# Three rounded passes for the query projections, the first context transposed in two halves, and a shorter first layer norm in a fused Perceiver layer

## The reference

```python
x = x + xattn(layernorm(x), ctx, ctx, Wq, Wk, Wv, Wo)   # 32 query heads, 8 key heads of 16, softmax over 512 keys
x = x + attn(layernorm(x), Wq, Wk, Wv, Wo)              # self-attention, rotary, causal, over 32 tokens
x = x + (layernorm(x) @ dequantised_3bit_W.T + bias)
```

## Time and profile before

| | |
|---|---|
| median of 3 runs | 363.48 us (362.62 to 363.76) |
| the profiled execution | 363.82 us |
| its span in the trace | 362.0 us |
| TensorE busy | 340.7 us, 94% |
| VectorE busy | 234.7 us, 65% |
| ScalarE busy | 201.6 us, 56% |
| GpSimd busy | 104.3 us, 29% |

### The profile page before, as it was taken

How to read it: one execution, slowest core, us unless ns; L and a number is a source line. 1 busy time by engine, 2 the same in 40 slices (tenths; PEclk the granted TensorE clock), 3 DMA queues, 4 the chain that set the end, 5 groups by cost and what they waited for, 6 DMA issues and landing times.

```text
span 362.0 us, 8407 instructions
## 1 busy us (share of the span) xinstructions
PE 340.7 (94%) x2958; PEld 243.1 (67%) x2962; DVE 234.7 (65%) x420; ACT 201.6 (56%) x371; POOL 104.3 (29%) x195
## 2 busy tenths in 40 slices
PE   8999778999999999999999999998798989999996
PEld 4755545777777777777777777775456748875664
DVE  2977655676676667666766766666856237886652
ACT  4543244567576675666675766758766522275310
POOL 1431812133131240331322412403103141551410
PEclk9999988999999999999999999999999999999999
DMA  7980497685876777869759686989600000000002
GB/s 282 394 94 4 92 208 172 159 101 162 141 138 149 110 177 159 109 168 175 99 154 163 116 173 125 205 196 122 84 0 2 2 0 2 1 2 0 2 29 87
DMA packets 35820, 41.25 MB, mean 114 GB/s; under 512 B 15136, under 2 KB 30496, under 8 KB 33696
## 3 DMA queue, kind: packets, MB, share of 16 engines
q1 hardware_dynamic: 35360, 40.74, 55.0%
q10 hardware_dynamic: 432, 0.13, 0.2%
HBM read 24.07 MB, written 1.05 MB: 69 GB/s over the span
## 4 chain that ended last, share of the span: by engine, by line
PE 82%; DVE 8%; DMA 2%; SPq 2%; ACT 2%; POOL 2%; issue 1%; ACTq 0%; DVEq 0%; POOLq 0%
PE b_d L1025 9%; PE b_s L1046 8%; PE b_c L1084 8%; PE b_v L1000 4%; PE b_c L1230 4%; PE b_v L1002 4%; PE b_v L1001 4%; PE b_k L1002 4%; PE b_k L1000 4%; PE b_k L1001 4%; PE b_x L972 3%; PE b_t L972 3%; DMA kstack<-kparts 2%; PE b_c L1215 2%; PE b_c L1111 2%; PE b_v L1051 2%
## 5 line engine op out<-in xcount | busy, mean ns | idle before, releaser
L758 DVE TENSOR_REDUCE negmax<-b_s 128x1 f32<-128x512 f32 x128 | 88.1, 688 | 67.1 <-PE b_s L1046 65.5
L610 ACT ACTIVATE region<-b_c 128x512 f32<-128x512 f32 x128 | 76.4, 598 | 60.9 <-PE b_c L1084 58.5
L1046 PE MATMUL b_s<-kstack,qstack 96*128 96x512 bf16 x128 | 50.2, 392 | 7.9 <-DVE negmax L758 3.5
L1084 PE MATMUL b_c<-qstack,kstack 108*128 108x128 bf16 x512 | 50.8, 222 | 0.3 <-ACT qstack L564 0.3
L1084 PEld LDWEIGHTS b_c<-qstack,kstack 108*128 108x128 bf16 x512 | 32.7, 98 | 26.5 <-issue 15.7
L469 POOL TENSOR_TENSOR mwide<-negmax,zeros 128x4 bf16<-128x4 f32 x32 | 6.4, 199 | 119.0 <-DVE negmax L758 119.0
L1025 PE MATMUL b_d<-region,vaug 128*17 128x128 f32 x1024 | 34.2, 274 | 0.0
L1000 PE MATMUL b_v<-cT_h,wkv_h 128*128 128x512 f32 x64 | 31.6, 494 | 0.0
L460 POOL TENSOR_TENSOR kparts<-kres,zeros 128x512 bf16<-128x512 f32 x16 | 18.9, 1179 | 44.0 <-DVE kres L743 44.0
L1000 PE MATMUL b_k<-cT_h,wkv_h 128*128 128x512 f32 x64 | 30.5, 476 | 0.0
L1025 PEld LDWEIGHTS b_d<-region,vaug 128*17 128x17 f32 x1024 | 25.2, 97 | 3.4
(11 more groups left out here) (395 smaller groups left out, 678.0 us busy)
## 6 DMA issues: line engine op xcount, KB each, us to landing
cx<-in_ctx_dram SPq DMA_DIRECT2D x16, 1024.0 KB, 5.2
kstack<-kparts SPq DMA_DIRECT2D x96, 128.0 KB, 4.6
qstack<-region SPq DMA_DIRECT2D x76, 32.0 KB, 3.6
xs<-in_x_dram SPq DMA_DIRECT2D x1, 1024.0 KB, 8.0
region<-in_L_xattn_Wq_dram SPq DMA_DIRECT2D x1, 1024.0 KB, 10.2
cx<-in_L_xattn_Wo_dram SPq DMA_DIRECT2D x8, 128.0 KB, 5.0
cx<-in_L_attn_Wq_dram SPq DMA_DIRECT2D x1, 1024.0 KB, 5.3
region<-in_L_attn_Wo_dram SPq DMA_DIRECT2D x8, 128.0 KB, 7.6
```

The lines of the kernel that those rows point to most:

```text
L610: nc.scalar.activation(pT[:, g], b_c[g % 2][:].rearrange("p (a n) -> p a n", a=KT), ACT.Exp, scale=SCALE).then_inc(exp_ready, 1)
L758: nc.vector.tensor_reduce(negmax[:, n % 2, g:g + 1], b_s[:], AX, ALU.max, negate=True).then_inc(max_ready, 1)
L1046: nc.tensor.matmul(b_s[:], qstack[0:STACK, g, n % 4], kstack[0:STACK, n % 4, g], start=True, stop=True).then_inc(s_ready, 1)
L1084: last = nc.tensor.matmul(b_c[g % 2][:, P * a:P * a + P], kstack[0:ROWS, m % 4, g, P * a:P * a + P], qstack[0:ROWS, g, m % 4], start=True, ...
```

## The change

Four edits, all in the openings.

1. The query projection takes three passes in the rounded format instead of one in fp32: `wq_h` by `xhT_h`, `wq_l` by `xhT_h`, `wq_h` by `xhT_l`, each over four chunks. The weights' high parts are copied into head order by ScalarE (chunk 0) and POOL (1, 2, 3); the low parts are subtracted by VectorE (0, 1) and POOL (2, 3), POOL's after all four tiles are normalised. The transposed rows' high parts are copied on ScalarE and their remainders subtracted on VectorE. The new operands lie in `wT_h`, `wT_l`, `swq_h` and `swq_l`, which are free until much later.
2. Context 0 is loaded in two halves of its row blocks, and transposed in two halves, with `warm(8)` ahead and `warm(2)` between, instead of `warm(14)`; both `warm(4)` are gone. The projections of context 0 wait chunk by chunk.
3. Epsilon becomes the bias of the square root.
4. The order changes. TensorE does query 0 ahead of the value transposes and of context 1, then queries 1 to 3 together, then chunks 2 and 3 of context 1. ScalarE and VectorE take those two chunks after all query parts, ScalarE also after its two DMA issues; VectorE unpacks the last piece (`unpack(5)`) after them, and does context 0's key remainder behind the row remainders.

```diff
+        wq_h, wq_l = (w[:].rearrange("p c (r n) -> p c r n", r=R) for w in (wT_h, wT_l))
+        xhT_h, xhT_l = swq_h, swq_l
+        b_rows = (b_c[1], b_t, b_x, b_s)
...
@@ SyncE, opening
+                halves = ctx_d[0].rearrange("(p a) d -> p a d", a=KT)
+                sp.dma_start(cx[:, 0, 0:2], halves[:, 0:2]).then_inc(first_half, 16)
                 sp.dma_start(wkv_raw[:, 0], xwk_d.rearrange("(c p) m -> p c m", p=P)).then_inc(wk_loaded, 16)
-                load_ctx(0, 0)
+                sp.dma_start(cx[:, 0, 2:4], halves[:, 2:4]).then_inc(ctx_loaded[0], 16)
...
@@ POOL, opening
+            nc.gpsimd.memset(eps[:], EPS).then_inc(eps_ready, 1)
...
                 pool.wait_ge(xwq_loaded, 16)
+                for c in (1, 2, 3):
+                    nc.gpsimd.tensor_copy(in_heads(wq_h, c), from_heads(xwq, c)).then_inc(wq_high[c], 1)
+                pool.wait_ge(xh_ready, TILES)
                 for c in (2, 3):
-                    nc.gpsimd.tensor_copy(wq_dg[:, c].rearrange("p r (d g) -> p r d g", g=G),
-                                          xwq[:, c].rearrange("p (g r d) -> p r d g", g=G, r=R)).then_inc(wq_ordered, 1)
+                    pool.wait_ge(wq_high[c], 1)
+                    nc.gpsimd.tensor_tensor(in_heads(wq_l, c), from_heads(xwq, c), in_heads(wq_h, c).bitcast(F32),
+                                            ALU.subtract).then_inc(wq_ready[c], 1)
...
@@ ScalarE, opening
-                act.wait_ge(ln1_var, 1)
-                nc.scalar.activation(rstd[:], mv[:, :, 1], ACT.Sqrt).then_inc(ln1_std, 1)
+                act.wait_ge(ln1_aggr, TILES)
+                act.wait_ge(eps_ready, 1)
+                nc.scalar.activation(rstd[:], mv[:, :, 1], ACT.Sqrt, bias=eps[:]).then_inc(ln1_std, 1)
                 act.wait_ge(xwq_loaded, 16)
-                nc.scalar.activation(wq_dg[:, 0].rearrange("p r (d g) -> p r d g", g=G),
-                                     xwq[:, 0].rearrange("p (g r d) -> p r d g", g=G, r=R), ACT.Copy).then_inc(wq_ordered, 1)
+                nc.scalar.activation(in_heads(wq_h, 0), from_heads(xwq, 0), ACT.Copy).then_inc(wq_high[0], 1)
+                for t in range(TILES):
+                    act.wait_ge(xh_transposed, t + 1)
+                    nc.scalar.activation(xhT_h[:, :, P * t:P * t + P], b_rows[t][:].rearrange("p (c n) -> p c n", c=C),
+                                         ACT.Copy).then_inc(xhT_high, 1)
                 act.wait_ge(v_chunk, C)
                 nc.scalar.activation(vT[:], b_v[:], ACT.Copy).then_inc(vT_ready, 1)
...
+                query_high(0)
                 context(1, 0)
                 context(1, 1)
-                query_high(0)
-                context(1, 2)
                 query_mid(0)
-                query_high(1)
-                context(1, 3)
-                query_mid(1)
-                for r in (2, 3):
+                for r in (1, 2, 3):
                     query_high(r)
                     query_mid(r)
                 act.wait_ge(q_mid, R)
                 first_queries_part(act, 1, 0, 1, first_queries)
+                context(1, 2)
+                context(1, 3)
                 key_high(1, 0)
...
@@ VectorE, opening
-                nc.vector.tensor_scalar(mv[:, :, 1], mv[:, :, 1], EPS, None, ALU.add).then_inc(ln1_var, 1)
...
+                for c in (0, 1):
+                    dve.wait_ge(wq_high[c], 1)
+                    nc.vector.tensor_tensor(in_heads(wq_l, c), from_heads(xwq, c), in_heads(wq_h, c).bitcast(F32),
+                                            ALU.subtract).then_inc(wq_ready[c], 1)
+                for t in range(TILES):
+                    dve.wait_ge(xhT_high, t + 1)
+                    nc.vector.tensor_tensor(xhT_l[:, :, P * t:P * t + P], b_rows[t][:].rearrange("p (c n) -> p c n", c=C),
+                                            xhT_h[:, :, P * t:P * t + P].bitcast(F32), ALU.subtract).then_inc(xhT_ready, 1)
                 key_residue(0, 0)
-                dve.wait_ge(xwq_loaded, 16)
-                nc.vector.tensor_copy(wq_dg[:, 1].rearrange("p r (d g) -> p r d g", g=G),
-                                      xwq[:, 1].rearrange("p (g r d) -> p r d g", g=G, r=R)).then_inc(wq_ordered, 1)
+                query_residue(0)
                 copy_values(0, 0)
                 context(1, 0)
                 context(1, 1)
+                query_low(0)
                 unpack(0)
                 unpack(1)
-                query_residue(0)
-                context(1, 2)
-                query_low(0)
+                query_residue(1)
+                query_low(1)
                 unpack(2)
                 unpack(3)
-                query_residue(1)
-                context(1, 3)
-                query_low(1)
-                unpack(4)
                 query_residue(2)
                 query_low(2)
-                unpack(5)
+                unpack(4)
                 query_residue(3)
                 query_low(3)
+                context(1, 2)
+                context(1, 3)
+                unpack(5)
                 key_residue(1, 0)
...
@@ TensorE
-                    if not looped(trip) and (m, c) == (1, 1):
-                        pe.wait_ge(xhT_ready, 1)
+                    if not looped(trip) and m == 1:
+                        pe.wait_ge(xhT_ready, TILES)
...
             def first_queries_of(r):
-                pe.wait_ge(xhT_ready, TILES)
-                pe.wait_ge(wq_ordered, C)
-                count(pe, q_res, r - 1)
-                for c in range(C):
-                    last = nc.tensor.matmul(b_c[r % 2][:], wq_dg[:, c, r], xhT[:, c], start=(c == 0), stop=(c == C - 1))
+
+                for i, (w, x, w_done) in enumerate(((wq_h, xhT_h, wq_high), (wq_l, xhT_h, wq_ready), (wq_h, xhT_l, wq_high))):
+                    pe.wait_ge((xhT_high, xhT_high, xhT_ready)[i], TILES)
+                    if i == 0 and r > 1:
+                        pe.wait_ge(q_res, r - 1)
+                    for c in range(C):
+                        pe.wait_ge(w_done[c], 1)
+                        last = nc.tensor.matmul(b_c[r % 2][:], w[:, c, r], x[:, c], start=(i == 0 and c == 0), stop=(i == 2 and c == C - 1))
                 last.then_inc(q_summed, 1)
...
             def opening():
                 pe.wait_ge(zeros_ready, 1)
-                warm(14)
+                warm(8)
                 pe.wait_ge(ident_loaded, 16)
-                first_context(0)
-                first_context(1)
-                first_context(2)
-                first_context(3)
-                warm(4)
-                pe.wait_ge(wk_split, 1)
+                pe.wait_ge(first_half, 16)
                 for c in range(C):
-                    project(0, 0, c, 0)
-                pe.wait_ge(wv_split, 1)
+                    first_context(c, (0, 1))
+                warm(2)
+                pe.wait_ge(ctx_loaded[0], 16)
                 for c in range(C):
-                    project(0, 1, c, 0)
-                warm(4)
+                    first_context(c, (2, 3))
+                pe.wait_ge(wk_high, 1)
+                first_projection(0)
+                pe.wait_ge(wv_high, 1)
+                first_projection(1)
...
+                first_queries_of(0)
                 pe.wait_ge(vT_ready, 1)
...
                 next_context(1, 0)
                 next_context(1, 1)
-                first_queries_of(0)
+                for r in range(1, R):
+                    first_queries_of(r)
                 next_context(1, 2)
-                first_queries_of(1)
                 next_context(1, 3)
-                first_queries_of(2)
-                first_queries_of(3)
                 for which in range(2):
                     for c in range(C):
                         project(1, which, c, 0)
```

More of the change, by code:

```diff
@@ L197, in perceiver @@
         scratch = kstack[:, 2:4].rearrange("p a g n -> p (a g n)").bitcast(F32)
+        eps = sb("eps_sb", [P, 1])
         qbytes = scratch[:, 0:3 * NTRIP].bitcast(I32).rearrange("p (n k) -> p n k", k=3)
         qvals = scratch[:, 3 * NTRIP:11 * NTRIP].bitcast(I32).rearrange("p (n k) -> p n k", k=8)
-        wq_dg = qstack[:].rearrange("p g i n -> p (g i n)").bitcast(F32).rearrange("p (c r n) -> p c r n", c=C, r=R)
+        wq_h, wq_l = (w[:].rearrange("p c (r n) -> p c r n", r=R) for w in (wT_h, wT_l))
+        xhT_h, xhT_l = swq_h, swq_l
         bits = scratch[:, 11 * NTRIP:15 * NTRIP].bitcast(I32).rearrange("p (k n) -> p k n", k=4)
@@ L251, in perceiver @@
             [sem(f"{name}{i + 1}") for i in range(2)] for name in ("ln_stats", "ln_aggr", "ln_var", "ln_std", "ln_rstd", "xn_ready"))
+        wq_high, wq_ready = ([sem(f"{name}{c}") for c in range(C)] for name in ("wq_high", "wq_ready"))
         ctx_loaded = [sem(f"ctx_loaded{i}") for i in range(2)]
@@ L307, in wait_queries, with in_heads, from_heads @@
                 eng.wait_ge(qstack_loaded[m % 4], 16 * SLOTS * (m // 4))
+        def in_heads(w, c):
+            return w[:, c].rearrange("p r (d g) -> p r d g", g=G)
```

(41 more changed lines are left out.)

20 lines of the change are left out of this document (7 added, 13 removed).

## The result

The changed kernel takes 366.58 us (median of 9 runs, 365.25 to 367.06) against 363.48: a ratio of 1.0077, with a 95% interval of 1.0053 to 1.0101. It is slower by 3.1 us, where 1.9 us of gain was forecast. Its profiled execution took 366.26 us with a span of 364.5, so it is 2.5 us longer than the span of 362.0 shown before.

The account below looks back on a forecast made before the run. TensorE, busy for 94% of the span, was taken as the bound, the change touching only the opening. Slot 1 0.35 us earlier plus 1.55 of half clock gone gave -1.9: 361.6 us against 363.48, range 358.2 to 365.2.

Parts of the forecast that it names:

- The mechanism named as likeliest: Opening: VectorE can't follow, TensorE waits 3.75 us for chunk 2, half clock follows, slot 1 at 55.7; 361.6 us, chance 0.42.
- The price of the passes: Query projections: 2.73 us a query in rounded products, 2.8 us of TensorE saved; queries 1 to 3 take 8.2.
- the first context: Context 0 in halves, fewer warming products: first chunk at about 7.4 against 7.45, taken as nothing, bounds -0.4 and +0.5.
- the normalising beside the copies: Layer norm: four tiles take 2.19 us on VectorE, not blocked by POOL's copies; rows end at 16.45.
- the half clock before slot 0: After TensorE's wait for chunk 2: 3.1 us at half clock, 1.55 us lost; slot 0 begins at 44.8.
- the tail: From slot 1 on nothing is touched, TensorE is busy to 97%, and the shift passes to the end.
- query 0 done: End of query 0's third pass: 23.2 us instead of 22.6, bounds 21.4 and 24.5.
- if the clock rises one stretch later: First context: bound of +0.5 us on its start, should TensorE's clock rise later.
- no turns: Rival on weight subtractions: no exclusion between VectorE and POOL, query 0 ends at 21.4; 358.9 us, chance 0.18.
- The rival "slower": Query 0's second and third pass: both POOL subtractions precede VectorE's second, TensorE's clock falls; 365.1 us, chance 0.14.
- That sign of the rival: A low clock between 20 and 27 us, named as what would show the slower rival (chance 0.14).
- The landing rival: Before slot 1: last key DMA issued at 47.2 takes 8.9 us again, slot 1 at 56.1; 363.5 us, chance 0.21.

Follow-up runs that it names:

- e4: Changed kernel with fifteen zero products in TensorE's wait for chunk 2 of context 1: 363.40 us, ratio 0.9985.
- e5: Changed kernel with ten zero products in TensorE's wait for the first self-attention rows at 261 us: 364.93 us, ratio 1.0033.
- e6: Kernel before with ten zero products in TensorE's wait for the first self-attention rows: 363.57 us, ratio 1.0010.
- e3: Changed kernel with chunks 2 and 3 of context 1 back between the queries on all three engines: 364.31 us, ratio 1.0013.
- e7: Changed kernel with GpSimd's three weight copies held until the rows are normalised: 367.98 us, one run.
- e8: Changed kernel with context 0 in one load and chunks 2 and 3 of context 1 back between the queries: 363.02 us, ratio 0.9980.
- e10: e8 with context 3's load issued early and ten zero products in the wait at 261 us: 358.94 us, ratio 0.9876 to the kernel before.
- e12: Kernel before with context 3's load issued early and ten zero products in the wait at 261 us: 359.45 us, ratio 0.9873.
- e9: Kernel before with context 3's load issued before SyncE waits for the query parts: 361.02 us, ratio 0.9944.

## Why the prediction was wrong, step by step

The mechanism named as likeliest was there: VectorE as the bound, a wait of 3.5 us (3.75 forecast) for chunk 2, a half clock after it, no wait for the keys and full clock into slot 1. That no key was waited for was forecast rightly: landed by 54, and by 55.8 at the latest in the trace. The price of the passes was right too: queries 1 to 3 take 8.3 us (26.57 to 34.87), where 8.2 was forecast. The sign was wrong because four terms were too small: the first context and the normalising beside the copies, which were taken at no loss, the half clock before slot 0, and the tail. In the profiled executions the forecast of -1.9 and the measured +2.5 differ by 4.4 us: 2.6 at 64 us and 1.8 in the tail. Of the 2.6, 2.4 are slot 1's start, and the rest is that the half clock of the kernel before behind slot 1 gave back 1.3 us instead of 1.55.

| step | forecast | measured | difference |
|---|---|---|---|
| first eviction | 7.65 | 8.59 | +0.94 |
| layer norm, from statistics to reciprocal | -0.38 | -0.34 | +0.04 |
| four tiles normalised | 2.19 | 3.42 | +1.23 |
| the four subtractions | 4.65 | 4.6 | 0 |
| query 0 done | 23.2 | 25.5 | +2.3 |
| low part of chunk 2 | 38.7 | 40.74 | +2.0 |
| from there to slot 0 | 6.1 | 7.14 | +1.0 |
| slot 0 | 10.9 | 10.17 | -0.7 |
| slot 1 begins | 55.7 | 58.11 | +2.4 |
| behind it | 0 | 1.8 | +1.8 |

*First context.* Taken at nothing, bound +0.5. The argument was that the same bytes had to be in as before. The runs show that they came in later (212 GB/s from 2 to 4 us against 320; key weights used at 6.48, not 3.88; second half at 8.1) and that two-part transposing costs 1.1 us even when they don't. The fall-back "if the clock rises one stretch later" was priced at +0.5; where it happened the eviction was at 9.5 to 9.9.

*Copies and normalising.* This was argued away in the rival "no turns": the normalising beside the copies "wasn't blocked". The row of four was a sum, and hid that one tile had taken 0.82 us and the others 0.53. In the old order the two overlapped for 0.5 us; in the new one the three copies (14.4 to 17.9) run beside most of the normalising (15.25 to 18.67). The Trainium skill's page "SBUF — State Buffer" (section "Who interferes with whom") says that VectorE's copy, cast and tensor_scalar can contend with GpSimd too, when they run in a mode that uses both ports, and not only instructions with two SBUF inputs. The prediction left that clause unused. The trace agrees with it (1.92 us alone, 3.42 beside three copies), though no run here shows the mode that the instruction ran in.

*The half clock before slot 0.* Priced at 3.1 us from two rows, it lasted 5.3 us after TensorE had resumed, 2.6 us of lost time instead of 1.55. e4 shows that this and nothing else stood between the low part of chunk 2 and slot 0.

*The tail.* "From slot 1 on nothing is touched" held for every instruction and failed for the clock. The wait at 261 us is the same 2.27 us in both, and filling it takes 1.65 us off one median and nothing off the other (e5, e6). No term or rival was made for it.

The rival "slower" had the right sign with the wrong place: GpSimd didn't take both its turns before VectorE's second, and the clock between 20 and 27 us was full. (In the profiled executions of e3 and e7 it was not: 0.50 for 6.8 us. That sign of the rival can come.) The landing rival was not what decided here, but it is what the kernel falls back to as soon as TensorE's own wait is removed (e3, e8). The chance of 0.19 for slower was too small for a change whose forecast gain of 1.9 us rested on a shift of 0.35 and a half clock going away, that is, for 1.55 us, on the clock.

## What to carry to other kernels

Saved work on the busiest engine counts only where it is waited for: e10 has 2.8 us less of it than e12, pays for that with splits on VectorE and GpSimd, and the two can't be told apart in time. Look for what an idle queue could have issued earlier; here one load moved across a wait gave 2.4 us. And keep short waits of TensorE filled: ten zero products, which no data depend on, were worth 1.6 us in two kernels and nothing in a third, and fifteen 3.2 us, of which the trace puts about half on a later dent that was gone. Look at the granted clock of the whole span when two kernels are compared, and not only where they differ.

## What the runs showed of the hardware

A wait of 2.27 us was followed by several microseconds of half clock in six of ten executions and by none in four, and the wait may lie far from any edit. Whether it is followed goes with the time at which it comes: 0.7 us later than in the kernel before it had a dent behind it (the changed kernel), 0.2 us later and 0.7 us earlier none (e3, e4), 4.75 us earlier one again (e9). TensorE was busy for 3.0 to 6.1 us in each of the low stretches of the openings.

A VectorE instruction with one tensor in SBUF and per-row scalars was held up by GpSimd's copies: up to 1.29 us for a tile of 0.54.

Issuing 512 KB ahead of the 256 KB of key weights moved these from 3.1 to 5.3 us to landing, for an issue 0.4 us later.
